# Rope attention with queries on partitions: scores once, maxima as the bias of the exponentials, exponentials turned by PE

## What is computed

```python
q = (x @ Wq).reshape(b, n, N_HEADS, HEAD_DIM)
k, v = jnp.split(ctx @ Wkv, 2, axis=-1)
...
q = apply_axial_rope(q, pos_map)
k = apply_axial_rope(k, ctx_pos_map)
scale = 1.0 / np.sqrt(HEAD_DIM).astype(np.float32)
logits = jnp.einsum('bqhd,bkhd->bhqk', q, k) * scale
w = jax.nn.softmax(logits, axis=-1)
attn = jnp.einsum('bhqk,bkhd->bqhd', w, v)
attn = attn.reshape(b, n, N_HEADS * HEAD_DIM)
return attn @ Wout + bout
```

## Time and profile before

| what | us |
|---|---|
| median of 3 runs (lowest, highest) | 2847.21 (2845.17, 2850.47) |
| the profiled execution, its own time | 2847.08 |
| span of the profiled execution | 2845.4 |
| PE busy | 2385.7 (84%) |
| PEld busy | 1803.0 (63%) |
| DVE busy | 1468.0 (52%) |
| ACT busy | 1070.1 (38%) |
| POOL busy | 719.7 (25%) |

### The profile page before, as it was taken

The page is one execution under the profiler, slowest core; times in us unless marked ns, Lnnn a source line. Parts: engine busy times, 40 slices in busy tenths (PEclk is TensorE's granted clock), DMA queues, the critical chain, the costliest instruction groups (busy, mean ns, idle before and its releaser), DMA issues. The chain is left out here.

```text
span 2845.4 us, 38555 instructions
## 1 busy us (share of the span) xinstructions
PE 2385.7 (84%) x12983; PEld 1803.0 (63%) x12983; DVE 1468.0 (52%) x2705; ACT 1070.1 (38%) x2281; POOL 719.7 (25%) x697
## 2 busy tenths in 40 slices
PE   2587777777874987999999999668999977499999
PEld 1454554554553976999999999524555544388887
DVE  5535434533545653566666666454655553644443
ACT  1233333333323321355555555315666553210110
POOL 2301211120121043144444444234444320000000
PEclk9867776776677998999999999878999987799999
DMA  7000000000002022588888988510000000300001
GB/s 270 12 1 5 5 0 5 5 1 4 5 1 96 35 40 79 167 232 247 244 234 235 244 242 234 132 68 8 5 5 5 1 1 1 133 1 0 0 0 59
DMA packets 139740, 217.63 MB, mean 76 GB/s; under 512 B 31496, under 2 KB 86408, under 8 KB 138373
## 3 DMA queue, kind: packets, MB, share of 16 engines
q1 hardware_dynamic: 111886, 166.34, 17.9%
q0 software_dynamic: 27712, 49.50, 9.0%
HBM read 168.00 MB, written 47.25 MB: 76 GB/s over the span
## 5 line engine op out<-in xcount | busy, mean ns | idle before, releaser
L2559 PE MATMUL d_Y<-d_mh,d_xT 128*128 128x512 f32 x1024 | 254.0, 390 | 13.0 <-DVE d_ml L2511 13.0
L1208 POOL DMA_INDIRECT b_y_rows<-b_ysb,b_entry x94 | 175.7, 1869 | 349.5 <-ACT b_ysb L1351 334.7
L1420 DVE TENSOR_TENSOR b_wl<-b_raw,b_wh 128x1472 fp32r<-128x1472 f32 x147 | 243.2, 1683 | 4.3 <-ACT b_wh L1343 4.3
L650 ACT ACTIVATE a_PT<-a_ST 128x512 f32<-128x512 f32 x256 | 149.5, 600 | 232.2 <-PE a_ST L740 231.7
L2559 PEld LDWEIGHTS d_Y<-d_mh,d_xT 128*128 128x128 f32 x1024 | 192.7, 188 | 53.3 <-issue 13.4
L1343 ACT ACTIVATE b_wh<-b_raw 128x1472 fp32r<-128x1472 f32 x147 | 205.3, 1437 | 1.6 <-DMA b_raw<-in_L_ffn_sd 1.6
L516 DVE TENSOR_REDUCE a_nm<-a_SM 128x2 f32<-128x512 f32 x256 | 166.6, 687 | 62.4 <-PE a_SM L734 61.8
L2515 DVE SCALAR_TENSOR_TENSOR X<-d_Y,d_gb,X 128x512 f32<-128x512 f32 x128 | 92.9, 752 | 171.1 <-PE d_Y L2559 171.0
L734 PE MATMUL a_SM<-a_kT,a_qT 48*128 48x256 f32 x512 | 149.0, 434 | 27.3 <-DVE a_nm L516 17.7
L434 POOL TENSOR_TENSOR a_rot<-a_rot,a_tmp 128x512 f32<-128x512 f32 x32 | 40.8, 1276 | 497.2 <-DVE a_tmp L493 497.2
L1902 DVE TENSOR_REDUCE c_nm<-c_SC 128x2 f32<-128x480 f32 x128 | 83.3, 651 | 151.4 <-PE c_SC L2159 150.9
(11 more groups left out here) (407 smaller groups left out, 5464.2 us busy)
## 6 DMA issues: line engine op xcount, KB each, us to landing
b_raw<-in_L_ffn_wg SPq DMA_DIRECT2D x47, 704.0 KB
b_raw<-in_L_ffn_wu SPq DMA_DIRECT2D x47, 704.0 KB
b_raw<-in_L_ffn_wd SPq DMA_DIRECT2D x47, 512.0 KB
b_raw<-in_L_ffn_wd SPq DMA_DIRECT2D x47, 192.0 KB
table<-st_zeros SPq DMA_DIRECT2D x4, 2048.0 KB, 21.1
d_M<-table SPq DMA_DIRECT2D x4, 2048.0 KB
X<-in_x SPq DMA_DIRECT2D x4, 1024.0 KB
b_xn_rows<-b_xg SPq DMA_DIRECT2D x16, 256.0 KB, 2.0
```

What stands on the lines that cost most here:

```text
L650: eng.activation(PT[:, h % (2 * QH), :, :].rearrange("p t s -> p (t s)"), ST[h % 2][:, :], ACT.Exp, scale=SCALE).then_inc(exp_done, 1)
L1208: eng.indirect_dma_start(out=y_rows, out_offset=bass.IndirectOffsetOnAxis(ap=entry[:, r % ENT, h, 1:2].bitcast(U32), axis=0), in_=ysb[:, v ...
L1420: eng.tensor_tensor(wl[s % 2][:, cols], raw[s % 2][:, cols], r32(wh[s % 2][:, cols]), ALU.subtract).then_inc(w_lo, 1)
L2559: m = eng.matmul(Y[t % NBANK][:, :], xT[x_][:, k, t * P:(t + 1) * P], w_[:, k, :], start=(i == 0), stop=(i == 3 * KD - 1))
```

## The change

rope_attention is written anew, and rope_tables gives the tables in a part of its own. There is no split of weights: products with weights are plain float32 (Wq is multiplied by the scale once, on DVE), and only q and k are split, into high and low parts of 16 dimensions each. A head has 32 rows, so that four heads stand in a tile of 128 rows; khT holds the high part of k twice, klT the low part twice, and a score is the sum of two products 32 rows deep. A slot is two heads: PE makes their scores with queries on partitions (8 matmuls of 256 columns), DVE takes both maxima, ACT makes four exponentials of 256 columns with the maximum as bias, each with its sum, PE turns them (8 transposes), and DVE and ACT copy one head each to PT. Every fourth slot PE turns the widened reciprocals and makes the weighted sum of 8 heads (16 matmuls); the bias of the output is a product more. Everything else of a batch is an item with a slot of its own (ITEMS_AT, counted from the batch's first slot), in a ring of three banks; the program is written out for all 128 slots, each engine going through the slots in its own order. Waits are on fixed counts of semaphores. filled, freed and is_freed are the waits of the ring; unit copies turned q or k to its tile, on ACT for q0a, q0b and the high parts of k, on DVE for the rest.

The core of the diff (added lines and those kept):

```diff
+    R = 2 * HD
     PAIRS = H // 2
+    HALF = PAIRS // 2
+    QUADS = H // 4
+    LEAD = 2
+    OH = 8
+    NO = H // OH
+    SLOTS = OH // 2
+    NP_, NPT = 4, 10
+    NW_ = 3
+    VW = 3 * HD
     SCALE = 1.0 / HD ** 0.5
+    END = B * PAIRS
+    ITEMS_AT = {-24: ("C", "X0", "X1"), -20: ("Q0",), -18: ("K0",), -16: ("Q1",), -14: ("K1",), -12: ("V0",), -11: ("V1",),
+                -9: ("q0a", "k0ha"), -8: ("k0la",), -7: ("q1a", "k1ha"), -5: ("k1la",), -2: ("q0b",), -1: ("q1b", "k0hb"),
+                1: ("k0lb", "k1hb"), 3: ("k1lb",), 22: ("O0",), 26: ("O1",)}
+    FIRST, LAST = -27, END + 27
+    TOKENS = -27
+    ROTATED = ("q0", "k0", "q1", "k1")
+    ROTATE_AT = {-19: 0, -17: 1, -15: 2, -13: 3}
+    HIGH_AT = {-17: 0, -15: 1, -13: 2, -11: 3}
+    LOW_AT = {-16: 0, -14: 1, -12: 2, -10: 3}
+    COLUMN_AT = {3: 0, 7: 1, 11: 2, 15: 3}
...
+        Pr = sb("P", [P, NP_, BT, S])
+        PT = sb("PT", [P, NPT, BT, S])
+        recw, recT = sb("recw", [P, 2, BT, OH, HD]), sb("recT", [P, 2, S])
+        aT = [sb(f"aT{i}", [P, NO, S]) for i in range(2)]
...
+        W = [ctx.enter_context(nc.psum_tensor(f"a_W{i}", [P, 512], F32)) for i in range(NW_)]
+        SC = [ctx.enter_context(nc.psum_tensor(f"a_SC{i}", [P, 512], F32)) for i in range(2)]
+        T_ = [ctx.enter_context(nc.psum_tensor(f"a_T{i}", [P, 512], F32)) for i in range(2)]
+        O = ctx.enter_context(nc.psum_tensor("a_O", [P, 512], F32))
...
+            def widened(n):
+
+                h = OH * (n % NO)
+                eng.wait_ge(rec_done, SLOTS * (n + 1))
+                ge(eng, weighted_done, n - 1)
+                eng.tensor_copy(recw[:, n % 2, :, :, :], rec[:, h:h + OH, :].rearrange("p h t -> p t h")
+                                .unsqueeze(3).to_broadcast([P, BT, OH, HD])).then_inc(rec_wide, 1)
...
+            def top(g, j):
+
+                eng.wait_ge(scored[j], g + 1)
+                eng.tensor_reduce(nm[:, g % 4, j, :], SC[j][:, :].rearrange("p (t k) -> p t k", t=BT),
+                                  AX.X, ALU.max, negate=True).then_inc(topped, 1)
+
+            def denominators(g):
+                h = 2 * (g % PAIRS)
+                for j in range(2):
+                    eng.wait_ge(exp_done[j], g + 1)
+                eng.reciprocal(rec[:, h:h + 2, :], den[:, h:h + 2, :]).then_inc(rec_done, 1)
+
+            def turned_back(g):
+                eng.wait_ge(turned[0], g + 1)
+                until_weighted(eng, g)
+                eng.tensor_copy(PT[:, 2 * g % NPT, :, :].rearrange("p t s -> p (t s)"), T_[0][:, :]).then_inc(pt_done[0], 1)
...
+            for s in range(FIRST, LAST):
+                if 0 <= s + 1 < END:
+                    top(s + 1, 0)
+                    top(s + 1, 1)
+                for b, n in items(s):
+                    if n[0] in "qk" and not by_scalar(n):
+                        unit(b, n)
+                for b, n in due(s, ROTATE_AT):
+                    rotate(b, n)
+                if 0 <= s < END:
+                    denominators(s)
+                if 0 <= s - 1 < END:
+                    turned_back(s - 1)
+                if s % SLOTS == 1 and SLOTS < s <= END + 1:
+                    normalise((s - SLOTS - 1) // SLOTS)
+                for b, n in due(s, LOW_AT):
+                    low_part(b, n)
+                for b, n in items(s):
+                    if n[0] == "O":
+                        add_out(b, int(n[1]))
...
+            def exponentials(g, j):
+                i = (2 * g + j) % NP_
+                h = 2 * (g % PAIRS) + j
+                eng.wait_ge(topped, 2 * g + j + 1)
+                ge(eng, turned[j], g - NP_ // 2 + 1)
+                for t in range(BT):
+                    e = eng.activation(Pr[:, i, t, :], SC[j][:, t * S:(t + 1) * S], ACT.Exp, bias=nm[:, g % 4, j, t:t + 1],
+                                       accum_out=den[:, h, t:t + 1])
+                e.then_inc(exp_done[j], 1)
+
+            def turned_back(g):
+                eng.wait_ge(turned[1], g + 1)
+                until_weighted(eng, g)
+                eng.activation(PT[:, (2 * g + 1) % NPT, :, :].rearrange("p t s -> p (t s)"), T_[1][:, :],
+                               ACT.Copy).then_inc(pt_done[1], 1)
...
+            for s in range(FIRST, LAST):
+                for b, n in items(s):
+                    if n[0] in "qk" and by_scalar(n):
+                        unit(b, n)
+                if 0 <= s + 1 < END:
+                    exponentials(s + 1, 0)
+                    exponentials(s + 1, 1)
+                if 0 <= s - 1 < END:
+                    turned_back(s - 1)
+                if s % SLOTS == 1 and SLOTS < s <= END + 1:
+                    turned_denominators((s - SLOTS - 1) // SLOTS)
+                for b, n in due(s, HIGH_AT):
...
+            def scores(g):
+                b, p = g // PAIRS, g % PAIRS
+                if p % HALF == 0:
+                    i = "ab"[p // HALF]
+                    for n in ("q0" + i, "q1" + i, "k0h" + i, "k0l" + i, "k1h" + i, "k1l" + i):
+                        is_freed(eng, (b, n))
+                for j in range(2):
+                    ge(eng, exp_done[j], g)
+                for t in range(BT):
+                    for half, k in enumerate((khT, klT)):
                         for j in range(2):
+                            r = R * (2 * (p % 2) + j)
+                            m = eng.matmul(SC[j][:, t * S:(t + 1) * S], qT[r:r + R, p // 2, t * P:(t + 1) * P],
+                                           k[r:r + R, p // 2, :], start=(half == 0), stop=(half == 1))
+                            if t == BT - 1 and half == 1:
+                                m.then_inc(scored[j], 1)
+
+            def turn_exponentials(g):
+                for j in range(2):
+                    eng.wait_ge(exp_done[j], g + 1)
+                    ge(eng, pt_done[j], g)
+                    for k in range(BT):
+                        for t in range(BT):
+                            m = eng.transpose(T_[j][:, k * S + t * P:k * S + (t + 1) * P],
+                                              Pr[:, (2 * g + j) % NP_, t, k * P:(k + 1) * P], core.ident[:, :])
+                    m.then_inc(turned[j], 1)
+
+            def weighted(n):
+
+                b, o = n // NO, n % NO
+                if o == 0:
+                    is_freed(eng, (b, "V0"))
+                    is_freed(eng, (b, "V1"))
+                ge(eng, att_ready, n)
+                eng.wait_ge(rec_wide, n + 1)
+                for j in range(2):
+                    eng.wait_ge(pt_done[j], SLOTS * (n + 1))
                 for t in range(BT):
+                    eng.transpose(O[:, S + t * P:S + (t + 1) * P],
+                                  recw[:, n % 2, t, :, :].rearrange("p h e -> p (h e)"), core.ident[:, :])
+                for k in range(BT):
+                    for odd in range(2):
+                        for j in range(4):
+                            h = OH * o + 2 * j + odd
+                            at = (h // 2) * VW + odd * HD
+                            m = eng.matmul(O[32 * j:32 * (j + 1), 0:S], V[b % 2][:, k, at:at + 2 * HD],
+                                           PT[:, (OH * n + 2 * j + odd) % NPT, k, :],
+                                           start=(k == 0 and odd == 0), stop=(k == BT - 1 and odd == 1))
+                m.then_inc(weighted_done, 1)
...
+                m.then_inc(weighted_done, 1)
+
+            for s in range(FIRST, LAST):
+                for b, n in items(s):
+                    item(b, n)
+                if s % SLOTS == 0 and SLOTS <= s <= END:
+                    weighted((s - SLOTS) // SLOTS)
+                if 0 <= s < END:
+                    turn_exponentials(s)
+                if 0 <= s + LEAD < END:
+                    scores(s + LEAD)
```

More of the change, by code:

```diff
@@ L404, in step @@
-            def step(b, last):
-                Wr = rings(b)[0]
-                for g in range(NG):
-                    eng.wait_ge(*Wr.until_freed(b, late(MAX_TR[g], last)))
-                    for par in range(2):
-                        for j in range(2):
-                            r = 4 * (2 * par + j)
-                            row = R * par + MAXROW + j
-                            eng.dma_start(r32(qT[row:row + 1, 4 * g:4 * g + 4, :]),
-                                          nmT[r:r + 4, g, :]).then_inc(max_rows[g], 16)
-                    if g == 0 and not last:
-                        context(b + 1)
@@ L421, in _ @@
+            eng.wait_ge(bias_set, 3)
+            eng.dma_start(r32(bias[1:2, :]), r32(blow[:, :])).then_inc(bias_in, 16)
+            for s in range(FIRST, LAST):
+                for b in range(1, B):
+                    if s - PAIRS * b == TOKENS:
+                        context(b)
         @block.gpsimd
         def _(eng):
[L423 to L425 removed]
@@ L451, in _, with tokens @@
-            for b in range(B):
-                step(b, b == B - 1)
+            eng.memset(one[:, :], 1.0).then_inc(consts, 1)
```

(64 more changed lines are left out.)

618 lines of the change are left out of this document (198 added, 420 removed).

## The result

| | us |
|---|---|
| before, median of 4 (lowest, highest) | 2847.61 (2845.17, 2850.47) |
| after, median of 4 (lowest, highest) | 2924.57 (2922.16, 2925.71) |
| ratio after / before, 95% interval | 1.0262 (1.0246 to 1.0278) |
| predicted | 2836 (2798 to 2905) |
| span of the profiled execution, before and after | 2845.4, 2924.0 |

The account below looks back on a forecast made before the run. No engine is full; a chain of waits bounds the rope attention. Start 95, plus 767 for slots (737, clock 30), plus tail 19.4, ends it at 881.5 against 892.5, 11 us less: 2836 us (2798 to 2905).

Parts of the forecast that it names:

- Start, 95: Rope attention's first scores come at 95 us (bounds 85 and 110), where the old first product starts at 124.84.
- Tail, 19.4: From the rope attention's last scores to its last sum: loop, turn, copy, weighted sum, normalising, outputs and sum, 19.4 us.
- Scores in tiles of 32 rows: A slot's 8 score matmuls, priced from the nearest rows, those of 64 rows: 0.67 us.
- rival 2: Scores in 32-row tiles cost twice 0.67 a slot if a pair's heads do not run together: +89, 2925 us; chance 0.07.
- The loop, 93.6 a batch at full clock: Chain scores, maxima, exponentials, ACT's copy, transposes, scores sets the slots: light 4.5, weighted about 7.45, 93.6 us a batch.
- The clock, 3.7 a batch, or 30 in all: PE's clock falls two to three times a batch after gaps in slots 13, 15, 1, 3: 3.7 us a batch.
- the bound from above, 12: Upper bound on the clock's cost a batch: all 12 light slots at 1.2 GHz, 1.0 us each.
- rival 1: Clock falls in the gaps around the four rotation slots and stays down: up to 12 us a batch, 2902; chance 0.25.
- The sister's 0.61 in thin slots: Granted clock in the last, gap-filled slots of the similarly built normed attention, 78% of time at 1.2 GHz; cited for rival 1.
- The rule on transposes: Trainium skill's statement that transposes do not engage full clock, so light slots, half transposes, would sink; the prediction doubted it.
- Rival 3: The clock stays up and the rope attention starts earlier, first scores at 88: 2799 us; chance 0.13.
- Rival 4: Copies and exponentials overlap, so PE's summed work, 64.7 us a batch, ends slots instead of the loop: 2587; chance 0.03.

Follow-up runs that it names:

- run 8: Changed kernel with extra unread matmuls in PE's gaps and 3 more behind slot 1's turned keys: 2830.4 us on another chip, ratio 1.0058 to the kernel before.
- Run 5: Changed kernel with both ACT and DVE copying the previous slot's turned exponentials before their other work of a slot: 2715.2 us, ratio 0.9533 to the kernel before.
- run 1: Changed kernel with 15 extra unread float32 matmuls a batch in PE's gaps, slot 1's left open: 2855.2 us, ratio 1.0021 to the kernel before.
- run 2: Changed kernel with extra unread transposes in PE's gaps, 8 in place of each matmul of run 1: 2853.7 us, ratio 1.0017 to the kernel before.

## Why the prediction was wrong

**Start, 95.** 99.0: 4 us late, within its bounds. DVE began the first rotation at 76.6 for 78, so the delay came behind it, in the first rotations and turns (22.4 us for 17). **Tail, 19.4.** 20.5 (last scores 950.3, end 970.7). Right.

**Scores in tiles of 32 rows.** Priced as those of 64 rows, 0.67, and so measured; rival 2 (2925) falls, though its number is nearly the result. The result has another cause.

**The loop, 93.6 a batch at full clock.** Right. The chain has the links and the length that the sum gave it (4.62 for 4.5), and in run 8, with the clock held, fifteen slots sum to 88.5 for 87.6. Slots with an output product are at 5.75 to the hundredth. Run 5 shows the loop from the other side: without the copies in it, 3.57.

**The clock, 3.7 a batch, or 30 in all.** This is the step that failed. Between first and last scores run 1 had 2 x 0.08 x 778 = 124 us at 1.2 GHz for 375, and took 73 us less (851.3 to 778.1): 0.29 us for each us of low clock, an estimate by which no low clock at all would give 851.3 - 0.29 x 375 = 742, where the prediction's slots sum to 737. So the clock cost about 109 us, 13.6 a batch, and not 30. Put in place of the prediction's term: 2836 + (109 - 30) + 4 (start) + 5 (slots) + 1 (tail) = 2925, the result; since 109 was taken from the measured stretch, this adds up by its making and tests nothing. A second way to the price comes near: against the same slots at 1.00 (in runs 1 and 8, and slot 1 in batch 4 of the changed kernel), the slots of batch 3 are longer by 1.6 (slot 0), 1.2 (slot 2), 1.5 (slot 4), 0.9 (slot 8), 2.2 (slot 12), 2.0 (slot 14) and 2.0 in slots 1, 7 and 11 together, 11.4 us for 38 at 1.2 GHz, 0.30 for each.

The mis-sizing has four parts. "Two to three falls a batch" were six in batch 3, with 38 us at 1.2 GHz. The sum of 3.7 takes 1.5 us for each fall, while 3 us of work at half the speed, as its words have it, would cost 3. "Loop work" is the wrong work: the falls run through slots 0, 2, 4, 8, 12 and 14, in which PE is busy to the end with a product or a weighted sum, so that the whole of PE's work stands on the path there, 1.5 us in slot 4 and 2.2 in slot 12. And the bound from above, 12, was made of light slots alone; by the estimate of 13.6 even the bound was passed. The argument used against rival 1, that a dense slot never lies more than two away, was the wrong way round: the clock did come back in or behind dense slots, but only after they had paid.

**Rivals.** Rival 1 is what happened: its sign was right, and its place for four of the six falls (those in slots 7 to 8 and 11 to 12 stand at gaps that it did not name). Its 2902 was short by 13.6 for 12 a batch (13 us) and by the 10 of start, slots and tail. The sister's 0.61 in thin slots and the 0.72 of the old stage itself were rows enough to give it more than 0.25. The rule on transposes that it names is not at work here, as it said (run 2). Rival 3 did not come up. Rival 4's 64.7 a batch was not reached even with both copies first (81.9, and 79.3 with extra matmuls), though PE then has the least room.

**What would show it.** Of the signs named as right, the light slots at 4.5 and the first scores were met, and the slots with a weighted sum only where the clock was up (7.29 in slot 8 of batch 4, at 1.00); the batches of 97 and the clock above 0.85 were not. None of the signs named as wrong came up: the clock, at 0.78, stayed just above their 0.75. ACT's copy is what ends the light slot, but over the whole stage DVE's copy is named more (148.3 us in 66 waits), as in the slots with a rotation.

Not tried: the kernel before with its clock held in the same way. So these runs do not tell how the two designs compare at full clock; they tell that the changed one needs 2855 us with its gaps mostly filled and 2715 with its copies in another order.
